# Row places computed and scattered by two tiles and two in a decoder layer with 160 experts

## What is computed

```python
x = _layernorm(x + _L0_attn_ref(x, ...))
x = _layernorm(x + _L0_xattn_ref(x, ctx_1024, ...))
logits = x @ router_w.T + expert_bias[None, :]        # 160 experts
top_w, top_idx = jax.lax.top_k(sigmoid(logits), 8)     # 8 for each token
h1 = silu(einsum('th,eih->eti', x, w_gate))            # 256 -> 128
routed = einsum('eti,ehi->th', h1 * combine, w_down)   # 128 -> 256
shared = silu(x @ w_gate_shared.T) @ w_down_shared.T
x = _layernorm(x + routed + shared)
```

## Time and profile before

| what | us |
|---|---|
| median of 3 runs | 903.7 |
| lowest, highest | 902.33, 905.53 |
| the profiled execution | 905.59 |
| its span in the trace | 903.5 |

### The profile page before, as it was taken

The page is one execution under the profiler, slowest core; times in us unless marked ns, Lnnn a source line. Parts: engine busy times, 40 slices in busy tenths (PEclk is TensorE's granted clock), DMA queues, the critical chain, the costliest instruction groups (busy, mean ns, idle before and its releaser), DMA issues. The chain is left out here.

```text
span 903.5 us, 14776 instructions
## 1 busy us (share of the span) xinstructions
PE 759.5 (84%) x3782; PEld 498.7 (55%) x3782; DVE 493.1 (55%) x1284; ACT 386.0 (43%) x809; POOL 361.9 (40%) x360
## 2 busy tenths in 40 slices
PE   7989999999996788897988940079999999999394
PEld 4654444444442457484755630058777777876273
DVE  1677778787752424757668288123433434432187
ACT  2346767767675243417153210025544444554011
POOL 9301010111000000036747777617777776777300
PEclk9989999999998699799998975579999999999698
DMA  6899787777745111023312223669999999996595
GB/s 242 291 349 308 224 296 253 271 273 241 288 164 188 37 46 48 24 98 130 132 70 97 109 102 131 243 170 371 370 374 368 373 372 345 359 366 219 232 422 212
DMA packets 103699, 208.05 MB, mean 230 GB/s; under 512 B 26024, under 2 KB 51666, under 8 KB 97377
## 3 DMA queue, kind: packets, MB, share of 16 engines
q1 hardware_dynamic: 64448, 129.53, 41.0%
q10 hardware_dynamic: 24320, 42.74, 13.4%
q0 software_dynamic: 14880, 35.17, 10.6%
HBM read 118.35 MB, written 96.08 MB: 237 GB/s over the span
## 5 line engine op out<-in xcount | busy, mean ns | idle before, releaser
L1741 POOL DMA_INDIRECT contributions<-c_c,e_dest x182 | 177.1, 973 | 85.2 <-ACT c_c L1722 43.6
L1892 POOL DMA_INDIRECT row_pool<-rows,places x128 | 132.0, 1031 | 160.6 <-issue 138.8
L542 DVE TENSOR_REDUCE a_mx<-a_psS 128x2 f32<-128x1024 f32 x128 | 152.0, 1218 | 31.3 <-PE a_psS L364 31.1
L500 ACT ACTIVATE a_e<-a_psT 128x512 f32<-128x512 f32 x256 | 135.5, 600 | 57.1 <-PE a_psT L394 52.2
L1696 DVE COPY e_xt<-e_psx 128x256 f32<-128x256 f32 (+1 forms) x130 | 68.6, 530 | 101.8 <-PE e_psx L1628 94.3
L1628 PE MATMUL e_psx<-m_c,rows 128*128 128x128 f32 x364 | 65.2, 286 | 67.8 <-PEq L677 63.1
L1642 PE MATMUL e_psg<-e_xt,e_w 128*128 128x64 f32 (+2 forms) x676 | 119.1, 309 | 1.8 <-issue 1.7
L1715 ACT ACTIVATE e_g<-e_psg 128x128 f32<-128x128 f32 (+1 forms) x130 | 41.7, 321 | 171.1 <-PE e_psg L1642 142.4
L1653 PE MATMUL e_psy<-e_w,e_g 128*128 128x256 f32 (+1 forms) x442 | 104.3, 394 | 0.0
L394 PE MATMUL a_psT<-a_q,a_k 128*128 128x512 f32 x256 | 98.5, 452 | 4.8 <-ACT a_e L500 3.0
L307 POOL MEMSET a_q<- 64x1024 f32 x32 | 30.3, 946 | 178.8 <-PE a_psT L394 177.7
(11 more groups left out here) (281 smaller groups left out, 967.8 us busy)
## 6 DMA issues: line engine op xcount, KB each, us to landing
row_pool<-fill SPq DMA_DIRECT2D x32, 1260.0 KB, 7.2
e_w<-w ACTq DMA_DIRECT2D x156, 256.0 KB
rows<-row_pool SPq DMA_DIRECT2D x143, 140.0 KB
c_c<-contributions SPq DMA_DIRECT2D x16, 1024.0 KB, 16.8
a_k<-k_parts SPq DMA_DIRECT2D x64, 128.0 KB, 3.4
rows<-row_pool SPq DMA_DIRECT2D x78, 70.0 KB
a_q<-q_parts SPq DMA_DIRECT2D x32, 128.0 KB, 4.1
a_q<-q_parts SPq DMA_DIRECT2D x64, 64.0 KB, 3.3
```

The lines of the kernel that those rows point to most:

```text
L500: nc.scalar.activation(E[:, i], psT[:, BANK[i]], ACT.Exp, scale=DH ** -0.5).then_inc(expd, 1)
L542: nc.vector.tensor_reduce(mx[:, at.slot, qt, 2 * DH * pair::HALF], psS[:, pair], AX, ALU.max).then_inc(maxed, 1)
L1741: nc.gpsimd.indirect_dma_start(out=contrib, out_offset=bass.IndirectOffsetOnAxis(ap=dest[:, result(f) + k:result(f) + k + 1], axis=0), in_ ...
L1892: nc.gpsimd.indirect_dma_start(out=pool, out_offset=bass.IndirectOffsetOnAxis(ap=place[:, b, t, k:k + 1], axis=0), in_=rows[:, b, t], in_o ...
```

## The change

`put` and `places` take a range of tiles and are called twice in each step, for the tiles 0 and 1 (`FIRST`) ahead of the merged weights `W1`, and for the tiles 2 and 3 (`OTHERS`) behind `PR`. `rows_done` is added to twice in each step, inside `places`, ahead of the update of `slots`. POOL scatters the tiles 0 and 1 on the first count with no wait between them, then waits for the second count, and then scatters 2 and 3, for the batches 0 and 1 behind the marks `x1t_done` and `um_done`, for batch 2 behind `mixed`, for batch 3 with no mark. In step 4 PE makes `rank` ahead of `share(0)`. SP loads only the 7 blocks of weights of the first half ahead of the end of `mix`. The row loads of the first half are shared out: SP issues the entries 0, 2 and 4 (5 DMAs), ACT the entries 1 and 3 (4 DMAs), each behind the same waits. The 6 blocks of weights of the second half are loaded by ACT at the start of `experts`, ahead of its first activation.

```diff
--- before.py
+++ after.py
@@ -101,6 +101,7 @@
 SHARED_AFTER = (2, 4, 4, 4)
 RING = 4
 HALF = P // 2
+FIRST, OTHERS = slice(0, TT // 2), slice(TT // 2, TT)
 
 
 def repeated(ap, at, count):
@@ -749,6 +750,12 @@
             for n in range(B + 1):
                 step(n, n < B, n > 0, n < B - 1)
 
+        def rows_sent(eng):
+            for r in range(2):
+                eng.wait_ge(sent[r], (B - r) // 2 * (16 * TT * TOP_K))
+            eng.wait_ge(shared_added, B)
+            eng.wait_ge(last_sent, 16 * TT * TOP_K)
+
         @block.sync
         def _(sp):
             def load_a(b):
@@ -776,16 +783,12 @@
             sp.dma_start(lists[:].rearrange("p e i -> p (e i)"),
                          repeated(listing.rearrange("e i -> (e i)"), 0, P)).then_inc(lists_in, 16)
             sp.wait_ge(tables_done, 1)
-            first = [tables.experts_of(0, h, mybir.EngineType.SP) for h in range(HALVES)]
+            first = tables.experts_of(0, 0, mybir.EngineType.SP)
+            for j in ENTRIES_OF[0]:
+                tables.load_weights(sp, w, j, first)
             first_pages = tables.pages_of(0, 0, mybir.EngineType.SP)
-            for j in range(RING_E):
-                tables.load_weights(sp, w, j, first[HALF_OF[j]])
-
-            for r in range(2):
-                sp.wait_ge(sent[r], (B - r) // 2 * (16 * TT * TOP_K))
-            sp.wait_ge(shared_added, B)
-            sp.wait_ge(last_sent, 16 * TT * TOP_K)
-            for j in ENTRIES_OF[0]:
+            rows_sent(sp)
+            for j in ENTRIES_OF[0][0::2]:
                 tables.load_rows(sp, pool, j, first_pages)
 
         @block.gpsimd
@@ -794,27 +797,24 @@
                 nc.gpsimd.memset(tile[:], 1.0).then_inc(ones_set, 1)
             pool_eng.sem_clear(spent)
             pool_eng.wait_ge(pool_filled, FILLS * 16)
-            for b in range(B - 1):
-                pool_eng.wait_ge(rows_done, b + 1)
-
+            for b in range(B):
+                here = sent[b % 2] if b < B - 1 else last_sent
+                pool_eng.wait_ge(rows_done, 2 * b + 1)
+
+                pool_eng.sem_inc(dispatching, 1)
+                dispatch(b, here, (0, 1))
+                pool_eng.wait_ge(rows_done, 2 * b + 2)
                 pool_eng.sem_inc(dispatching, 1)
                 if b + 2 < B:
-                    dispatch(b, sent[b % 2], (0,))
-                    pool_eng.wait_ge(x2t_done, b + 2)
-                    dispatch(b, sent[b % 2], (1,))
                     pool_eng.wait_ge(x1t_done, b + 3)
-                    dispatch(b, sent[b % 2], (2,))
+                    dispatch(b, here, (2,))
                     pool_eng.wait_ge(um_done, b + 3)
-                    dispatch(b, sent[b % 2], (3,))
+                    dispatch(b, here, (3,))
+                elif b + 1 < B:
+                    pool_eng.wait_ge(mixed, TT * B)
+                    dispatch(b, here, (2, 3))
                 else:
-                    dispatch(b, sent[b % 2], (0,))
-                    pool_eng.wait_ge(mixed, TT * B)
-                    dispatch(b, sent[b % 2], (1, 2))
-                    pool_eng.wait_ge(routed, B)
-                    dispatch(b, sent[b % 2], (3,))
-            pool_eng.wait_ge(rows_done, B)
-            pool_eng.sem_inc(dispatching, 1)
-            dispatch(B - 1, last_sent, range(TT))
+                    dispatch(b, here, (2, 3))
             for r in range(2):
                 pool_eng.wait_ge(sent[r], (B - r) // 2 * (16 * TT * TOP_K))
 
@@ -891,9 +891,9 @@
                 tile = lambda t: n * TT + (t + 1)
                 if not part_b:
                     gate(3)
-                    share(0)
                     pe.wait_ge(shared_silu, 3)
                     rank(n)
+                    share(0)
                     share(1)
                     pe.wait_ge(ranks_read, B)
                     for b in range(2, B):
@@ -1062,6 +1062,11 @@
                     for b in range(B):
                         act.wait_ge(shared_gated, b + 1)
                         nc.scalar.activation(GS[:, b], ps[:, GATES[b]], ACT.Silu).then_inc(shared_silu, 1)
+                    act.wait_ge(tables_done, 1)
+                    first_pages = tables.pages_of(0, 0, mybir.EngineType.Activation)
+                    rows_sent(act)
+                    for j in ENTRIES_OF[0][1::2]:
+                        tables.load_rows(act, pool, j, first_pages)
                     return
                 if part_a:
                     copy_heads(n + 1)
@@ -1199,18 +1204,21 @@
                     do(nc.vector.tensor_tensor(shift2[:], shifts[:, b], last_shift[:], ALU.subtract))
                     o2.hold()
 
-                def put():
-                    do(nc.vector.scalar_tensor_tensor(step1[:], rank[:], float(P), repeated(shift1[:], 1, TT), ALU.is_ge, ALU.mult))
-                    do(nc.vector.tensor_tensor(step2[:], rank[:], repeated(limit[:], 1, TT), ALU.is_ge))
-                    sync()
-                    do(nc.vector.tensor_tensor(step2[:], step2[:], repeated(shift2[:], 1, TT), ALU.mult))
-                    do(nc.vector.tensor_tensor(rank[:], rank[:], step1[:], ALU.add))
-                    sync()
-                    do(nc.vector.tensor_tensor(rank[:], rank[:], step2[:], ALU.add))
-                    sync()
-                    do(nc.vector.tensor_tensor(key[:], repeated(C[:, COL["far"]], 1, TT), rank[:], ALU.subtract))
-                    sync()
-                    do(nc.vector.tensor_tensor(key[:], key[:], mask[:], ALU.mult))
+                def put(ts):
+                    some_rank, one, two_, own_key = rank[:, ts], step1[:, ts], step2[:, ts], key[:, ts]
+                    count_of = ts.stop - ts.start
+                    every = lambda a: repeated(a, 1, count_of)
+                    do(nc.vector.scalar_tensor_tensor(one, some_rank, float(P), every(shift1[:]), ALU.is_ge, ALU.mult))
+                    do(nc.vector.tensor_tensor(two_, some_rank, every(limit[:]), ALU.is_ge))
+                    sync()
+                    do(nc.vector.tensor_tensor(two_, two_, every(shift2[:]), ALU.mult))
+                    do(nc.vector.tensor_tensor(some_rank, some_rank, one, ALU.add))
+                    sync()
+                    do(nc.vector.tensor_tensor(some_rank, some_rank, two_, ALU.add))
+                    sync()
+                    do(nc.vector.tensor_tensor(own_key, every(C[:, COL["far"]]), some_rank, ALU.subtract))
+                    sync()
+                    do(nc.vector.tensor_tensor(own_key, own_key, mask[:, ts], ALU.mult))
                     o2.hold()
 
                 def keep():
@@ -1222,14 +1230,15 @@
                         do(nc.vector.tensor_tensor(shift1[:], shift1[:], moved[:], ALU.add))
                         do(nc.vector.tensor_tensor(last_shift[:], last_shift[:], moved[:], ALU.add))
 
-                def places():
-                    for t in range(TT):
+                def places(ts):
+                    for t in range(ts.start, ts.stop):
                         do(nc.vector.max(k8[:, t], key[:, t]))
                     o2.hold()
-                    do(nc.vector.tensor_scalar(place[:, n - 1], k8[:], -1.0, FAR, ALU.mult, ALU.add))
-                    do(nc.vector.tensor_copy(rows[:, n - 1, :, CODES:NAMES], slots[:]))
-                    sync()
-                    do(nc.vector.tensor_scalar(slots[:], slots[:], float(S * TOP_K), None, ALU.add))
+                    do(nc.vector.tensor_scalar(place[:, n - 1, ts], k8[:, ts], -1.0, FAR, ALU.mult, ALU.add))
+                    do(nc.vector.tensor_copy(rows[:, n - 1, ts, CODES:NAMES], slots[:, ts]))
+                    sync()
+                    dve.sem_inc(rows_done, 1)
+                    do(nc.vector.tensor_scalar(slots[:, ts], slots[:, ts], float(S * TOP_K), None, ALU.add))
 
                 def list_entries():
 
@@ -1429,7 +1438,8 @@
                     nc.vector.tensor_scalar(ng[:], ps[:, 4, P:P + 1], -1.0, None, ALU.mult).then_inc(ng_done, 1)
                 if part_c:
                     grow()
-                    put()
+                    put(FIRST)
+                    places(FIRST)
                 if part_b:
                     dve.wait_ge(hc_summed, n + 1)
                     do1(nc.vector.tensor_reduce(esum[:], ps[:, 4, 2 * P:2 * P + TT], AX, ALU.add))
@@ -1444,15 +1454,13 @@
                         last = nc.vector.scalar_tensor_tensor(W1[:, c], Wqv[:, 3 * DC + c], hc[:, c:c + 1], Wqv[:, c],
                                                               ALU.mult, ALU.add)
                     last.then_inc(w1_done, 1)
-                if part_c:
-                    places()
-                    dve.sem_inc(rows_done, 1)
-                if part_b:
                     for c in range(DC):
                         dve.wait_ge(hq_done, DC * n + (c + 1))
                         last = nc.vector.tensor_tensor(PR[:, c], HQ[:, c], X1T[:, c], ALU.mult)
                     last.then_inc(pr_done, 1)
                 if part_c:
```

(5 more changed lines are left out.)

## The result

| | before | changed |
|---|---|---|
| median, us | 903.02 (901.82 to 905.53, 4 runs) | 895.91 (895.13 to 897.33, 4 runs) |
| the profiled execution, us | 905.59 | 895.13 |
| its span, us | 903.5 | 893.1 |

The ratio is 0.9922, interval 0.990 to 0.9945: 7.1 us faster. The forecast was 895.5, faster, with a range of 892.5 to 901.0. The total was right. The terms behind it were not all right, and their errors cancelled, which is what the experiments had to bring out.

The account below looks back on a forecast made before the run. POOL, having begun late, was taken to bound the end of `mix`, and with it PE's start in `experts`. Terms -3.3 - 3.0 - 2.2 + 0.3 = -8.2 took the median from 903.7 to 895.5 us, range 892.5 to 901.0.

Parts of the forecast that it names:

- The last scatter: End of `mix`: with places by halves, POOL's last scatter starts 3.3 us earlier, at 578.0; bounds 0 and 5.3.
- +0.3, charged to POOL: Steps 1 and 2: POOL issuing under the layernorm chains costs 0.3 us per step; the last step starts 0.3 later.
- The stretching: Batch 3: `put(OTHERS)` on DVE running beneath POOL's scatters lengthens them by 1.0 us in all.
- Rival 3: Nothing stretches POOL: the last scatter starts 4.9 us earlier, gain 9.8, time 893.9; chance 0.08.
- `rank` first: Step 4 on PE: making `rank` ahead of `share(0)` gains 0.7 us.
- Landing: End of `mix`: with 7 blocks of weights, SP starts about 2.6 us after the last scatter instead of 5.63, 3.0 earlier.
- Issue: Row loads at the end of `mix`: SP's five take 3.2 us instead of 5.40 for nine, 2.2 earlier.
- rival 4: ACT, not SP, is last at the meeting of engines and scatters land late all the same; about 901.7; chance 0.05.
- The six blocks in `experts`: Start of `experts`: weights loaded by ACT fall into a nearly empty DMA stretch and cost 0.3 us.
- Rival 1: `experts` pays 4.2 us for the moved weights: gain 4.3, time 899.4; chance 0.15.
- rival 2: End of `mix`: the last batch doesn't start earlier; gain 4.9 us, time 898.8; chance 0.13.
- rival 5: Slower: late silus or weights in `experts` keep PE's clock low, costing 11.3 us against 8.5; chance 0.04.

Follow-up runs that it names:

- e8: Changed kernel with only tile 0 in the first part for batches 2 and 3, without batch 2's pacing wait; 894.84 us.
- e6: Changed kernel with POOL's old wait for `x2t_done` put back between tiles 0 and 1 of batches 0 and 1; 898.19 us.
- e1: Kernel before with only places and scatters by halves and `rank` ahead of `share(0)`; 13 blocks of weights and all nine row loads on SP; 899.98 us.
- e11: Changed kernel with all 13 blocks of weights on SP ahead of the landing again, row loads still shared; 899.01 us.
- a1: Changed kernel run once more without any edit, giving the second profile; 896.12 us.
- e5: Changed kernel with `share(0)` ahead of `rank` again in step 4; 895.75 us.
- e7: Changed kernel with only 4 blocks of weights by SP and the other 9 by ACT at the start of `experts`; 895.53 us.
- e9: e8 with 4 blocks of weights ahead of the rows; at the start of `experts` SP loads three more ahead of its rows, ACT six; 894.80 us.
- e10: e8 with 4 blocks of weights ahead of the rows and the other nine loaded by ACT at the start of `experts`; 893.67 us.
- e2: Kernel before with the changed loads alone: six blocks of weights moved to ACT in `experts`, row loads shared by SP and ACT; 896.30 us.
- e3: Kernel before with only the six second-half blocks of weights moved to ACT at the start of `experts`; 900.06 us.
- e4: Kernel before with only the nine row loads shared out, 5 on SP and 4 on ACT; 900.60 us.

## Why the prediction was right, point by point

**The last scatter: -3.3 predicted, -4.3 and -4.9 measured.** The half `put` is what it was said to be. DVE's timeline of the changed kernel in step 3:

```profile
486.10 0.49 DVE L1211 SCALAR_TENSOR_TENSOR m_step<-m_rank,m_shift 128x320 f32<-128x320 f32 x1
...
489.64 0.55 DVE L1235 MAX8 m_k<-m_rep 128x8 f32<-128x160 f32 x2
...
499.38 0.76 DVE L582 BATCH_NORM_STATS2 m_st<-m_ps 128x6 f32<-128x256 f32 x2
504.86 0.76 DVE L582 BATCH_NORM_STATS2 m_st<-m_ps 128x6 f32<-128x256 f32 x2 [4.72 <-PE m_ps L977]
```

0.49 an instruction, 489.64 - 486.10 = 3.54 for the half, and the first statistics right behind `keep`, with 4.72 of idle time before the second pair: late and hidden, as written. What was off lies around it.

Counted from step 1, the last scatter's -4.26 has three pieces: batch 2 starts 2.95 earlier (118.78 to 115.83), its 32 scatters take 42.24 instead of 44.48, and the 31 behind batch 3's first take 42.54 instead of 41.61. In the second profile the pieces are -2.90, -2.24 and +0.20. The prediction, counted in the same way, had batch 2 at 114.3, batch 3 at 159.0 and the last scatter at 201.6. Batch 2 came 1.6 later than that, batch 3 0.9 earlier. Of the 2.24 within batch 2 it used 1.6 (32 x 1.34 = 42.9) without naming it: in the kernel before 1.44 of extra idle time stood ahead of the ninth scatter of that batch, where POOL waits for the mark `mixed`, and 0.8 more in longer instructions.

*Batch 2 later: steps 1 to 3 take 106.8 from count to count instead of 105.4* (the four kernels with whole places: 105.4 to 105.5; those with halves: 106.8; e8: 104.0). I had +0.3, charged to POOL. e6 has POOL's old pace and the same 106.80, so that reason is wrong. It arises between the first count and the second (54.1 instead of 52.3). 0.3 of that stands ahead of the router's matmuls (L992), in e6 too; the rest is twelve matmuls of the cross attention, in the kernel before:

```profile
415.15 5.42 PE L910 MATMUL m_ps<-m_ct,m_et 128*128 128x512 f32 x12 [1.54 <-ACT m_et L1015]
```

and in the changed kernel:

```profile
414.66 7.11 PE L910 MATMUL m_ps<-m_ct,m_et 128*128 128x512 f32 x12 [1.81 <-ACT m_et L1015]
```

The granted clock over 415 to 422 us was 1.00 and 0.76. Between the second count and the third it is the other way round for these matmuls (7.11 before, 5.42 changed), but the eight of L942 take 6.5 to 6.6 instead of 5.40; that way takes 52.7 instead of 53.1. e8 has 5.42 and 5.40.

*Batch 3 earlier: the next step takes 41.2 instead of 44.95*, where nothing was predicted but the 0.7 of `rank`. The eight matmuls of L942 in step 3, kernel before:

```profile
482.48 6.50 PE L942 MATMUL m_ps<-m_at,m_cr 128*128 128x512 f32 x8 [0.69 <-ACT m_at L1040]
```

the changed kernel:

```profile
482.94 3.70 PE L942 MATMUL m_ps<-m_at,m_cr 128*128 128x512 f32 x8 [0.69 <-ACT m_at L1040]
```

and e1:

```profile
481.20 5.40 PE L942 MATMUL m_ps<-m_at,m_cr 128*128 128x512 f32 x8 [0.69 <-ACT m_at L1040]
```

The granted clock over 480 to 490 us was, in the kernel before:

```profile
480.00:490.00 10.00, 8.65 (x26) 4.63 (x26) 9.17 (x21) 1.78 (x4) 7.86 (x8) 0.66 0.33 112
```

and in the changed kernel:

```profile
480.00:490.00 10.00, 8.02 (x36) 5.11 (x37) 8.61 (x26) 2.06 (x5) 7.87 (x8) 1.00 0.36 118
```

So 2.8 us came off PE's work; 2.4 of them reach DVE's logits, and the wait of 1.40 is gone too. But little of this reaches the scatters, since in the changed kernel batch 3 is held by POOL alone. In e1 and e11 the matmuls take 5.40, the step takes 42.3 to 42.4, batch 3 waits for its places, and it starts all the same at 158.10 and 158.11 (158.07 and 158.12 in the changed kernel). With the 6.50 of before, e1's places would come 1.1 later and batch 3 with them (an estimate: 6.50 - 5.40). So about 1 us of the 2.8 reaches the path, as much with 5.40 as with 3.70, and it is the 0.9 by which batch 3 comes before its forecast.

*The stretching: +1.0 predicted.* +0.93 (42.54 against 41.61) in the first profile looks like it, but is luck. `put(OTHERS)` runs from 531.74 to 535.1 and stretches two scatters, to 1.16 and 1.15: by 0.37 together, and one of the two still belongs to batch 2. The rest are mostly single scatters of 1.40 to 1.72 later in the batch, past `put`, and they change from profile to profile: the 31 take 40.97 to 42.25 with whole places and 41.72 to 42.54 with two tiles first (seven profiles), 41.81 in a1. So the price of `put` on POOL was put too high, by two thirds. Rival 3, nothing stretches POOL, falls as a mechanism, for 1.15 and 1.16 stand under the half `put`, less than the 1.29 to 1.62 under the whole one; but its number for the last scatter (4.9 earlier) is that of the second profile.

The Trainium skill's page "SBUF — State Buffer", section "Who interferes with whom", infers that tensor_tensor doesn't hold up descriptor writing; the same section says that a tensor_tensor with both inputs in SBUF contends with what GpSimd reads there. The 1.15 under a half `put`, which is six tensor_tensor and one scalar_tensor_tensor, against 0.97 alone fits the second sentence, since a scatter reads its `places`. It doesn't decide about the first, and which of the seven instructions does it was not told apart.

Whether the clock pattern is caused by the halves, I can't say. In step 3 it was the same in six profiles (changed, a1, e5, e7, e9, e10: 3.70), but e1, e6 and e11, with the same halves, have 5.40, and the kernels with whole places have 6.4 to 6.5. And e8 differs from the others in step 1 already, ahead of anything that its edit touches. It is no simple consequence of one edit and may change from execution to execution. That stays open.

**`rank` first: -0.7 predicted, 0 measured.** e5 shows it. The step of the argument that failed is that PE was taken at the clock of before: at 2.4 GHz the wait of 1.40 is gone in either order. In e1 and e11, where PE is at 1.2 GHz there, `rank` first saves DVE about 1.0. That is more than the 0.7, because `rank` starts 0.15 after the mask is made (519.71 against 518.74 + 0.82 in e1) and not 0.5.

**Landing: -3.0 predicted, -2.3 and -0.9 measured.** The mechanism was right: e2, e3 and e11 show that the queued weights hold the last scatters. "Drained by 578" came out, but not as worked out: the tables come 2.3 earlier instead of 0.7 later (SP's first weights 195.66 and 193.34 after the count), so the seven blocks are issued by 572.9 and not by 576, and still the DMA engines fall to 0.41 only after 578 and to 0.00 after 579. What I left out is that my own first term works against it. The earlier the last scatter, the more of the weights it meets: of 4.4 won there e1 gives back 1.2, and even with seven blocks 0.7 (3.37 against 2.71) or 2.1 (4.78) are lost. The terms of a sum were taken as independent where they share the DMA engines.

**Issue: -2.2 predicted, -2.1 measured,** in e4 alone as in the whole: 7.07 to 4.97. ACT was not the last at the meeting, so rival 4 falls.

The Trainium skill's page "DMA: Bandwidth & Descriptors", section "Issuing engines are not separate DMA queues", gives the time of the issuing as all that there is to be won; e4 agrees, its landing is 5.67 as before.

**The six blocks in `experts`: +0.3 predicted.** PE's start to the end takes 309.5, 309.7, 307.0 and 308.0 with all 13 blocks ahead, and 305.9 to 308.6 with seven (307.4 over seven kernels). Rival 1's 4.2 is excluded. The +0.3 itself is too small to be seen in this. The first silu isn't even late: 588.26 - 584.66 = 3.60 after PE's start, as before (597.60 - 594.00), since ACT issued its six loads at 0.48 each, not 0.60. In e3 they took 3.32 and the silu came 0.55 late; nine loads (e7, e10) delay it by 2.5 to 2.7.

**Rivals 2 and 5.** Batch 3 starts 5.2 earlier counted from step 1, so rival 2 falls. The clock rises no later (0.74 over PE's first 10 us), so rival 5 falls.

**The sum.** On the path from step 1's count to PE's start: -4.26 - 2.26 - 2.10 = -8.6 in the first profile and -4.94 - 0.85 - 2.09 = -7.9 in the second, against -8.5. It was right, in part by luck: the last scatter came 1.0 and 1.6 earlier than forecast (0.9 from batch 3's start, by a clock that was not foreseen, 0.1 and 0.8 from POOL's 31 others), and the meeting of scatters and weights took 0.7 and 2.1 away again. Medians gave 7.1 and 5.9, and 7.2 for e5, which runs like the changed kernel.

## What to carry to other kernels

When two parts of a change shorten neighbouring links of one chain, ask whether the earlier link's gain brings the next one into a busy stretch. Here scatters that start 4 us earlier meet the weights that SP has queued, and 0.7 to 2.1 us go back; the version with the lowest median (e10) moved the bulk loads out of the way at the same time. A wait in a profile, such as DVE's 1.40 for `rank`, may be worth nothing to an edit: here it was about 1.0 with PE at 1.2 GHz and nothing at 2.4. And time that an engine saves counts only up to where the next one is free: of 2.8 us off PE's work in step 3 about 1 reached batch 3, because POOL was still busy. Before crediting an edit with what one profile shows, look whether the difference begins before the edit acts, as it did in e8.

## What the runs showed of the hardware that I had not expected

- From the last scatter's start to the release of SP it takes 2.7 us once the queued weights have drained (e2, e3), and up to 6.8 with 13 blocks of 256 KB queued (e1). With seven blocks it went from 2.71 to 5.56 as the last scatter's start came from 10.5 to 2.8 us after the first of them.
- The stretch of `mix` in which PE is granted 1.2 GHz changed from kernel to kernel, and once (e8) between kernels that had done the same up to there. From 482.9 to 486.6 us the granted clock was 0.50 in the kernel before and 1.00 in the changed one. The same eight matmuls took 3.70, 5.40 or 6.5 us, twelve others 5.42 or 7.11. Of 2.8 us gained in this way on PE about 1 reached the scatters.
- ACT issues six loads of weights in 2.86 (0.48 each; 3.32 in e3) and nine in 5.29 to 5.42 (0.59 to 0.60 each).
- POOL's scatter instruction takes 0.97 alone, 1.15 to 1.16 under DVE's half `put` (128x320) and 1.29 to 1.62 under the whole one (128x640).
